# One accumulator for the experts' outputs in a transformer layer with 64 experts, and another division of its last stage

## What is computed

```
x = x + _layernorm(_L0_attn_ref(_layernorm(x), Wq, Wk, Wv, Wo))
x = x + _layernorm(_L0_ffn_ref(_layernorm(x), gate_w, gate_up_proj, down_proj, shared...))

# _L0_ffn_ref, for T = 4096 tokens, E = 64 experts, K = 6 a token, at most CAP = 128 rows each
scores = softmax(xf @ gate_w.T); topk_w, topk_idx = top_k(scores, K)
gx = xp[buf_tok]                                  # (E, CAP, 512)
g, u = split(einsum('ech,ehi->eci', gx, gate_up_proj))
eo = einsum('eci,eih->ech', silu(g) * u, down_proj) * buf_w[..., None]
routed = zeros((T + 1, h)).at[buf_tok.reshape(-1)].add(eo.reshape(-1, h))[:T]
shared = silu(xf @ shared_gate_w.T) * (xf @ shared_up_w.T) @ shared_down_w.T
return routed + shared
```

## Time and profile before

| | |
|---|---|
| median of 3 runs | 2278.55 us (2272.32 to 2315.87) |
| profiled execution | 2303.76 us, of which the span is 2301.7 us |
| granted TensorE clock over the span | 0.921 |
| experts, first to last issue of an addition | 1857.0 to 2210.2 us |
| last stage | about 2215 to 2302 us |

### The profile page before, as it was taken

One profiled execution on the slowest core, in us unless ns is written; L12 is line 12 of the kernel. 1 busy time (PEld: TensorE's weight loads), 2 busy tenths in 40 slices (PEclk: granted clock), 3 DMA queues, 4 the chain that ended last, 5 costly groups with the idle time before them and its releaser, 6 DMA issues.

```text
span 2301.7 us, 41702 instructions
## 1 busy us (share of the span) xinstructions
PE 1964.9 (85%) x12707; PEld 976.5 (42%) x12707; DVE 1314.6 (57%) x2831; ACT 1042.5 (45%) x1568; POOL 718.4 (31%) x985
## 2 busy tenths in 40 slices
PE   6999979989999799889997979899979688998930
PEld 3434335544333355543343545334345344444410
DVE  4588836546798265468982654688736312222248
ACT  2557753334677433446774334567733222222200
POOL 2212214522222145222222452122215422222248
PEclk9889989987899899979998999799989899999975
DMA  2122323310000121100001110000002199999988
GB/s 84 55 93 94 127 87 111 137 54 2 11 16 12 33 98 67 38 6 11 12 12 42 62 59 21 6 12 12 16 28 75 62 300 322 335 335 315 339 252 293
DMA packets 108130, 232.81 MB, mean 101 GB/s; under 512 B 24423, under 2 KB 24423, under 8 KB 107920
## 3 DMA queue, kind: packets, MB, share of 16 engines
q1 hardware_dynamic: 81072, 191.07, 23.9%
q0 software_dynamic: 24576, 35.07, 6.3%
q10 hardware_dynamic: 2272, 4.06, 0.5%
HBM read 141.59 MB, written 126.48 MB: 116 GB/s over the span
## 4 chain that ended last, share of the span: by engine, by line
PE 59%; DVE 12%; issue 10%; DMA 7%; ACT 3%; POOL 2%; DVEq 2%; SPq 1%; another core or an unknown queue 1%; POOLq 1%; ACTq 0%
PE ps L759 9%; DVE rmax L1212 8%; PE ps L698 7%; PE ps L653 6%; DMA gx<-dispatch_scratch 6%; PE ps L898 5%; PE ps L845 4%; PE ps L779 4%; PE ps L871 3%; PE ps L930 3%; PE ps L884 3%; PE ps L654 3%; PE ps L673 2%; PE ps L872 2%; PE ps L705 2%
## 5 line engine op out<-in xcount | busy, mean ns | idle before, releaser
L1212 DVE TENSOR_REDUCE rmax<-ps 128x1 f32<-128x512 f32 (+3 forms) x1280 | 732.5, 632 | 188.0 <-PE ps L708 114.2
L1038 ACT ACTIVATE pr<-ps 128x1024 f32<-128x1024 f32 (+3 forms) x768 | 586.2, 813 | 239.4 <-PE ps L779 233.2
L698 PE MATMUL ps<-kT,qT 48*128 48x512 f16 (+3 forms) x1536 | 396.5, 349 | 34.0 <-DVE rmax L1212 23.8
L759 PE MATMUL ps<-pr,v_ones 128*32 128x512 f32 (+3 forms) x3072 | 348.1, 528 | 7.9 <-POOL pr L1488 4.5
L1488 POOL TENSOR_SCALAR_AFFINE_SELECT pr<-pr 128x512 f32<-128x512 f32 x256 | 162.2, 638 | 502.5 <-ACT pr L1038 501.1
L779 PE MATMUL ps<-qT,kT 50*128 50x512 f16 (+3 forms) x1536 | 301.4, 344 | 17.0 <-ACT pr L1038 7.9
L698 PEld LDWEIGHTS ps<-kT,qT 48*128 48x128 f16 x1536 | 123.3, 95 | 343.8 <-DVE rmax L1212 282.8
L1534 POOL DMA_INDIRECT dispatch_scratch<-x,slot_i x192 | 190.1, 990 | 73.4 <-issue 73.4
L705 PE MATMUL ps<-above,sel 64*128 64x128 bf16 x1024 | 190.1, 227 | 0.0
L898 PE MATMUL ps<-gu_sb,gxT 128*128 128x384 f32 x512 | 189.0, 493 | 0.0
L1553 POOL DMA_INDIRECT acc_scratch<-eo,etok x64 | 98.7, 1541 | 282.5 <-DVE eo L1351 270.3
(11 more groups left out here) (149 smaller groups left out, 2599.0 us busy)
## 6 DMA issues: line engine op xcount, KB each, us to landing
gu_sb<-w_gu_dram SPq DMA_DIRECT2D x64, 768.0 KB, 7.6
dn_sb<-w_dn_dram SPq DMA_DIRECT2D x64, 384.0 KB, 9.0
dispatch_scratch<-blank SPq DMA_DIRECT2D x8, 2308.0 KB, 8.8
gx<-dispatch_scratch SPq DMA_DIRECT2D x64, 288.5 KB, 5.2
xin<-x_dram SPq DMA_DIRECT2D x32, 256.0 KB
acc_scratch<-blank SPq DMA_DIRECT2D x32, 256.0 KB, 2.1
xres<-x_dram SPq DMA_DIRECT2D x32, 256.0 KB
x_scratch<-x SPq DMA_DIRECT2D x32, 256.0 KB, 2.0
```

The source lines that it names most:

```text
L698: last = pe.matmul(o, qT[r:r + SROWS, half, 2 * g + h // 2, q % QPH * P:(q % QPH + 1) * P], kT[r:r + SROWS, g, kh * HALF:kh * HALF + w], s ...
L759: last = pe.matmul(ps[32 * h:32 * h + 32, 6, c0:HALF], v_ones[g % 2][:, kt, :], pr[i % SLOTS][:, h, 0:HALF - c0], start=kt == 0, stop=kt = ...
L1038: act.activation(pr[i % SLOTS][:, 2 * pair:2 * pair + 2, 0:HALF - c0], ps[:, 2 + 2 * pair:4 + 2 * pair, 0:HALF - c0], ACT.Exp, scale=facto ...
L1212: dve.tensor_reduce(dst[:, heads[0] % 2, heads[0] // 2:heads[0] // 2 + n, q % QPH], ps[:, BANK_OF[item], 0:n * w].rearrange("p (h k) -> p ...
```

## The change

There is one accumulator, `acc_d`. `acc2_d` is gone, and with it its 32 clearing writes in SP's queue, the second write of blank rows by ScalarE at the start, the loads of `fz` and the addition of the two in the last stage. All 64 additions go to `acc_d` and count on one semaphore, so each waits until the addition of the expert just before has landed.

The last stage has 16 buffers `fy` in place of six pairs, and all 16 loads are issued at once. VectorE computes mean and variance; ScalarE adds EPS, negates the mean and subtracts it from both halves of a tile (`centre`); the lower half is scaled and added to `x1_all` by one instruction on VectorE, the upper half is scaled by ScalarE and added to `x1_all` by GpSimd. The tile is stored from `fy` itself.

```diff
                 def clear(g):
-                    sp.dma_start(acc2_t[bass.ds(TT * b + g, 1)].squeeze(0), blank[:, 0:D]).then_inc(acc_blank, 16)
...
-            def load_f(j, k):
-                sp.dma_start(fy[k][:], acc_f[j]).then_inc(f_in[k], 16)
-                sp.dma_start(fz[k][:], acc2_f[j]).then_inc(f_in[k], 16)
...
+            for j in range(FIN):
+                sp.dma_start(fy[j][:], acc_f[j]).then_inc(f_in[j], 16)
+            for j in range(FIN):
+                sp.wait_ge(low_out, j + 1)
+                sp.wait_ge(high_out, j + 1)
+                sp.dma_start(out_f[j], fy[j][:]).then_inc(f_out, 16)
...
+            def centre(j):
+                k = j % 2
+                act.wait_ge(fmv_ready, j + 1)
+                act.activation(fvr[:, k, :], fmv[:, k, :, 1], ACT.Copy, bias=EPS).then_inc(fvr_ready, 1)
+                act.activation(fnm[:, k, :], fmv[:, k, :, 0], ACT.Copy, scale=-1.0)
+                act.drain()
+                for f in range(FT):
+                    last = act.activation(fy[j][:, f, :], fy[j][:, f, :], ACT.Identity, bias=fnm[:, k, f:f + 1])
+                last.then_inc(centred, 1)
+
+            centre(0)
+            for j in range(FIN):
+                if j + 1 < FIN:
+                    centre(j + 1)
+                act.wait_ge(frs_ready, j + 1)
+                act.drain()
+                act.activation(fy[j][:, 1, :], fy[j][:, 1, :], ACT.Copy, scale=frs[:, j % 2, 1:2]).then_inc(scaled, 1)
...
                 if not first:
-                    dve.wait_ge(added[k % 2], 16 * (2 * i + k // 2 - 1))
+                    dve.wait_ge(added, 16 * (4 * i + k - 3))
...
             def f_stats(j):
                 k = j % 2
-                fb = fy[j % FB]
-                dve.wait_ge(f_in[j % FB], 32 * (j // FB + 1))
-                dve.tensor_tensor(fb[:], fb[:], fz[j % FB][:], ALU.add)
+                dve.wait_ge(f_in[j], 16)
+                for f in range(FT):
+                    dve.bn_stats(fst[:, k, f, :], fy[j][:, f, :])
                 dve.drain()
                 for f in range(FT):
-                    dve.bn_stats(fst[:, k, f, :], fb[:, f, :])
-                dve.drain()
-                for f in range(FT):
-                    dve.bn_aggr(fmv[:, k, f, :], fst[:, k, f, :])
-                dve.drain()
-                dve.tensor_scalar(fvr[:, k, :], fmv[:, k, :, 1], EPS, None, ALU.add).then_inc(fvar_ready, 1)
+                    last = dve.bn_aggr(fmv[:, k, f, :], fst[:, k, f, :])
+                last.then_inc(fmv_ready, 1)
...
                 dve.wait_ge(frs_ready, j + 1)
-                for f in range(FT):
-                    last = dve.tensor_scalar(fy[j % FB][:, f, :], fy[j % FB][:, f, :], fmv[:, k, f, 0:1], frs[:, k, f:f + 1],
-                                             ALU.subtract, ALU.mult)
-                last.then_inc(fn_ready, 1)
+                dve.wait_ge(centred, j + 1)
+                dve.scalar_tensor_tensor(fy[j][:, 0, :], fy[j][:, 0, :], frs[:, k, 0:1], x1_all[:, FT * j, :],
+                                         ALU.mult, ALU.add).then_inc(low_out, 1)
...
             with pool.Fori(1, E // 4) as i:
                 for k in range(4):
-                    pool.wait_ge(added[k % 2], 16 * (2 * i + k // 2))
+                    pool.wait_ge(added, 16 * (4 * i + k))
                     add_rows(4 * i + k, k)
...
+            f_root(0)
+            for j in range(FIN):
+                if j + 1 < FIN:
+                    f_root(j + 1)
+                pool.wait_ge(scaled, j + 1)
+                pool.tensor_tensor(fy[j][:, 1, :], fy[j][:, 1, :], x1_all[:, FT * j + 1, :], ALU.add).then_inc(high_out, 1)
```

More of the change, by code:

```diff
@@ L422, in program @@
         FT = 2
-        FB = 6
-        fy = [sb(f"fy{k}", [P, FT, D], f32, fi) for k in range(FB)]
-        fz = [sb(f"fz{k}", [P, FT, D], f32, fi) for k in range(FB)]
+        FIN = T // (P * FT)
+        fy = [sb(f"fy{j}", [P, FT, D], f32, fi) for j in range(FIN)]
         fst = sb("fst", [P, 2, FT, 6], f32, fi)
         fmv = sb("fmv", [P, 2, FT, 2], f32, fi)
+        fnm = sb("fnm", [P, 2, FT], f32, fi)
         fvr = sb("fvr", [P, 2, FT], f32, fi)
@@ L472, in program @@
         eht_done, ehT_copied, edn_done, eo_ready = sem("eht_done"), sem("ehT_copied"), sem("edn_done"), sem("eo_ready")
[L473 removed]
+        added = sem("added")
         x1_back = sem("x1_back")
[L475 to L477 removed]
+        f_in = [sem(f"f_in{j}") for j in range(FIN)]
+        fmv_ready, fvr_ready, frs_ready = sem("fmv_ready"), sem("fvr_ready"), sem("frs_ready")
+        centred, scaled = sem("centred"), sem("scaled")
+        low_out, high_out, f_out = sem("low_out"), sem("high_out"), sem("f_out")
         block = ctx.enter_context(nc.Block())
@@ L500, in program @@
         acc_t = acc_d.rearrange("(n p) d -> n p d", p=P)
-        acc2_t = acc2_d.rearrange("(n p) d -> n p d", p=P)
         @block.sync
@@ L952, in _ @@
             act.wait_ge(const_ready, 1)
-            for rows_past in (acc_d, acc2_d):
-                act.dma_start(rows_past[T:T + CAP], blank[:, 0:D]).then_inc(acc_blank, 16)
+            act.dma_start(acc_d[T:T + CAP], blank[:, 0:D]).then_inc(acc_blank, 16)
             act.drain().then_inc(pv_copied, 1)
@@ L1553, in add_rows @@
                 pool.indirect_dma_start(
-                    out=(acc_d, acc2_d)[k % 2], out_offset=bass.IndirectOffsetOnAxis(ap=etok[k][:], axis=0),
-                    in_=eo[k][:], in_offset=None, bounds_check=T + CAP - 1, compute_op=ALU.add).then_inc(added[k % 2], 16)
-            pool.wait_ge(acc_blank, 16 * (2 + NT))
+                    out=acc_d, out_offset=bass.IndirectOffsetOnAxis(ap=etok[k][:], axis=0),
+                    in_=eo[k][:], in_offset=None, bounds_check=T + CAP - 1, compute_op=ALU.add).then_inc(added, 16)
+            pool.wait_ge(acc_blank, 16)
             for k in range(4):
-                if k >= 2:
-                    pool.wait_ge(added[k % 2], 16)
+                if k >= 1:
+                    pool.wait_ge(added, 16 * k)
                 add_rows(k, k)
```

41 lines of the change are left out of this document (8 added, 33 removed).

## The result

| | before | after |
|---|---|---|
| median | 2297.21 us (4 runs, 2272.32 to 2326.33) | 2451.92 us (4 runs, 2442.29 to 2458.96) |
| profiled execution, its span | 2303.76 us, 2301.7 us | 2446.97 us, 2445.2 us |
| granted TensorE clock over the span | 0.921 | 0.908 |
| additions, first to last issue | 1857.0 to 2210.2: 353.2 us | 1825.8 to 2380.1: 554.3 us |
| last addition's issue to the end | 91.5 us | 65.1 us |

The changed kernel is slower: the ratio is 1.0755, with an interval of 1.0687 to 1.0823. The forecast was 2413 us, with a range of 2336 to 2500. Every ratio in this document compares fast runs alone (those within 1.5% of the fastest of their kernel), while the medians beside it are over all runs, so a ratio isn't the quotient of the two medians.

The account below looks back on a forecast made before the run. The experts were taken to run at the edge of both DMA engines and TensorE. From 2303.8 us, +157 (experts) and -22 (last stage) gave 2438.8, less 25.2 for a slow profiled run: 2413 us, range 2336 to 2500.

Parts of the forecast that it names:

- The chain of additions: Experts' stage: each addition waits for the previous landing, a period of 8.26 us against 5.61, costing +157 us; chance 0.72.
- Its latency: Experts' stage: an addition among loads takes 7.4 us from issue to landing, as the first did; 4.86 us alone.
- The turnaround: GpSimd in the experts' stage: 0.86 us added to an addition's latency to give the period.
- The sign at GpSimd: Changed profile: GpSimd's idle time should end with an addition's landing, not VectorE's output; additions about 8.3 us apart.
- The last stage: Last stage: a tile falls from 4.27 to 2.9 us, -22 us in all, bounds -11 and -32.
- the 32 us that the prediction named as a sign of being wrong: Last stage: the prediction is wrong if this stage gives back more than 32 us.
- The clearing writes: SP's queue in the batches: dropping the 32 writes was put at 0 us, bounds 0 and -7.4.
- The frame: Whole kernel: 2438.8 us for the profiled execution, less 25.2 us by which it exceeded the median, 2413.5 us.
- Additions that stay hidden: Rival, experts' stage: latency at its lower bound, period 5.72 us, +7 us there, 2263 us in all; chance 0.11.
- the estimate of 2.6 us for an addition: Skill page's DMA latency: a period of 3.5 us, no cost to the experts, 2257 us in all.
- Half the clock: Rival, experts' stage: TensorE at 1.2 GHz throughout needs 10.3 us an expert, 2553 us in all; chance 0.06.
- Contention of the whole kind: Rival, experts' stage: latency stays at 9.0 us, period 9.86, +251 us there, 2519 us in all; chance 0.08.

Follow-up runs that it names:

- e1_one_acc: Kernel before with all 64 additions sent to the first accumulator, each waiting for the previous landing; second accumulator still cleared and read: 2498.07 us, ratio 1.0879.
- before_again: Kernel before, unchanged, profiled once more on one chip beside the unchanged changed kernel: 2272.10 us.
- the second pair of profiles: Kernel before and changed kernel, both unchanged, profiled once more on one chip: 2272.10 and 2445.39 us.
- e8_dve_both: Changed kernel with both halves of a last-stage tile scaled and added by VectorE, GpSimd left with the root: 2461.55 us, ratio 1.0766.
- e3_clear_once: Kernel before with the second accumulator cleared in the first batch only, by 8 larger writes: 2346.05 us, ratio 1.0217.
- e7_x1_spread: Kernel before with x1_all loaded as 128 KB after every expert in place of 512 KB after every fourth: 2277.19 us, ratio 0.9964.
- e6_loads_later: Changed kernel with SP waiting for a 64-byte DMA before it issues the loads of expert e + 4: 2359.96 us, ratio 1.0322.
- e2: Changed kernel with additions to two accumulators again, the second neither cleared nor read, so odd experts are left out: 2314.87 us, ratio 1.0059.

## Why the prediction was right, point by point

**The chain of additions.** Right, and the only cause of the loss (e1_one_acc). `gx` left the chain: in after it lands 2.9 us after its issue in the set beside the addition at 1889.21, where the earlier trace rows have 5.15. The DMA share was predicted at about 0.7 and is 0.71.

**Its latency: the term that was too small.** 7.4 us was taken from the first addition. In after the mean of the first 59 is 8.1 us, the median of all 8.0. The turnaround, 0.86, was read from the end of an output to the issue; from a landing to the issue it is 0.93. The last ones, without loads, are 5.6 to 6.5 us apart; 5.72 was forecast. The term that was mis-sized is the latency, and the step behind it is "I take 7.4 us, the first addition, since the new chain repeats its situation". The chain did repeat a situation, but that of all additions of before, whose median was 8.2 us (before_again); the first was a short one among them. In the trace of before the silence ahead of its first packet is 4.5 us and the median of all 64 is 4.9; from its issue to its last packet it took 7.1 us, and the median is 7.9. Why the first is shorter, no run shows. 59 x (9.0 - 8.26) = 44 us, which is the difference between 201 and 157; about 39 of them are latency and 5 turnaround. The addition of the earlier trace rows, at 8.1 to 9.0 us, was nearer to the usual one than the first, which was taken.

**The sign at GpSimd.** The prediction said that its idle time should end with a landing and not with VectorE's output. The profile names the output 58 times; by the count of outputs it was the landing, as forecast.

**The last stage.** Predicted -22 us with a bound at -32, measured -26.4 and, in the second pair of profiles, -33.5. The second lies just past the 32 us that the prediction named as a sign of being wrong. The tile of 2.9 us was met (about 3). Two of its terms were off: the new instruction was put at 0.61 us and takes 0.74 alone (e8_dve_both), and the transfers were put at 324 GB/s, to which they weren't held. In 40 slices of 2405 to 2445, after moves

```profile
GB/s 391 385 379 387 391 389 399 412 404 401 418 401 416 399 387 281 324 33 182 350 0 119 389 16 199 326 0 143 377 4 213 311 0 170 354 0 170 367 387 125
```

near 400 GB/s while the loads last, and then waits for tiles to store: VectorE, busy for 45.2 of the 50 us from 2390 to 2440, is the bound, not the DMA engines. That VectorE and GpSimd would exclude each other was listed as a suspicion from the earlier trace rows, and e8_dve_both shows it.

**The clearing writes.** Predicted 0; e3_clear_once gives nothing, and e7_x1_spread, which has them all, begins its additions as early as after.

**The frame.** The sum for the profiled execution was 2438.8 us and it took 2446.97. That closeness is luck: 44 us too little in the experts were nearly made up by 31 us in the batches, for which the sum has 0. The step from there to 2413, minus 25.2 us because the profiled run of before lay above the median, was sound: about 23 us of that run belonged to its conditions. So the 39 us between 2413 and 2451.92 are the real miss, and 44 us of experts less the 4 to 12 us that the last stage gave beyond the forecast account for it.

**The rivals.** Additions that stay hidden: refuted, their latency is far above 5.9 us; the estimate of 2.6 us for an addition, by the Trainium skill, page "DMA: Bandwidth & Descriptors", section "Anatomy of one DMA", isn't met even by the shortest, 4.6. Half the clock: the granted clock of the stage did fall, from 1.00 in before's long stretch to 0.86, but TensorE had slack for it and isn't in the chain. Contention of the whole kind: refuted with a latency of 9.0 us, though it was the right side to lean to; what additions in the full stream take, 8.2 us, is what they take in the chain.

## What to carry over

Take a DMA's latency from all its instances in the trace and not from one: the first addition took 7.4 us, the usual one 8.2, and that was most of the error in the experts. A latency that nothing waits for costs nothing until a change lets something wait for it: the second accumulator, which let two additions overlap, was worth 8.8% here (e1_one_acc). Where one landing releases a small DMA and a large set of loads, their order and distance set the small one's latency, and moving the loads by a few microseconds gave back 4.3 of the change's 7.5%. A releaser that the profile names may only end at the right time: count whether it is the one that the wait is about. Compare profiles that were taken beside each other, since about 23 us of a difference between two profiles had nothing to do with the code.

## What the hardware showed that I had not expected

- An accumulating indirect DMA of 0.26 MB is silent for 2 us alone and for 5 us beside a fresh set of loads of 1.44 MB, and its latency goes from 4.75 to 8.0 us; its first packet moves 4.4 to 5.0 us after the issue of the 768 KB load in that set, even if the addition is issued up to 2.5 us later than the load (e6_loads_later), and with the loads 1.75 to 2.45 us ahead the median period is 6.6 us in place of 9.0.
- `SCALAR_TENSOR_TENSOR` on half a tile takes 0.74 us on VectorE alone and up to 1.82 beside GpSimd's `TENSOR_TENSOR` (1.26 us).
- Four waits of ScalarE of about 8.6 us, 34 us in all, appear in six of the profiles and in eight others not, though the programs there are the same; their cause is open.
- The experts' stage with two accumulators took from 343 to 402 us; in the long ones (e2, e3) the `gx` issued behind `x1_all` lands after 8.3 and 7.7 us at the median, where before_again has 5.3, and in the one looked at TensorE's granted clock is 0.50 after it.
